# A mixer stage rebuilt with channels on the partitions, and a reordered expert stage

## The reference

```
x = x + attention(norm(x))   # 16 heads, top 128 of 512 scores kept, three powers
x = x + experts(norm(x))     # 8 experts, capacity 512 tokens each
x = x + mixer(norm(x))       # a state space mixer
x = x + experts(norm(x))     # the same weights again
```

```
z, xBC, dt = split(u W_in)                      # 128, 160 and 8 columns
dt = softplus(dt + dt_bias)
x, B, C = split(silu(causal_conv4(xBC) + conv_b))
a = -exp(A_log) * dt                            # a log decay for each token and head
y[l] = sum_{s<=l} (C[l].B[s]) exp(sum_{s<r<=l} a[r]) dt[s] x[s]   # for each head
y = concat(y + D x, z)                          # 256 channels
y = (y - mean) / sqrt(var + 1e-5) * ln_w + ln_b
out = y W_out.T
```

## Time and profile before

| what | us |
|---|---|
| median of three runs | 2978.61 |
| the profiled execution: its time | 2989.87 |
| the profiled execution: its span | 2988.0 |
| attention and set-up, up to about | 2347 |
| first experts, about | 2347 to 2480 |
| mixer, about | 2480 to 2899 |
| second experts, about | 2899 to 2988 |

### The profile page before, as it was taken

One profiled execution on the slowest core, in us unless ns is written; L12 is line 12 of the kernel. 1 busy time (PEld: TensorE's weight loads), 2 busy tenths in 40 slices (PEclk: granted clock), 3 DMA queues, 4 the chain that ended last, 5 costly groups with the idle time before them and its releaser, 6 DMA issues. The chain is left out here.

```text
span 2988.0 us, 55735 instructions
## 1 busy us (share of the span) xinstructions
PE 2555.0 (86%) x16480; PEld 1495.8 (50%) x16480; DVE 2633.9 (88%) x6567; ACT 2087.5 (70%) x6347; POOL 2273.3 (76%) x2876
## 2 busy tenths in 40 slices
PE   5888888888888888888988888888887786889868
PEld 3444444444444444444444444444444445777754
DVE  7999999999999999999999999999998354655537
ACT  4788888888888888888887888888887253222325
POOL 5899999989999999999999999999998242222205
PEclk7899999999999999999999999999999786655569
DMA  4444444444444444444444444444442000000000
GB/s 130 117 121 118 123 121 120 120 121 121 120 122 119 122 119 124 119 121 119 122 119 121 121 123 118 122 122 120 124 121 82 1 1 15 8 4 4 1 1 29
DMA packets 368965, 281.82 MB, mean 94 GB/s; under 512 B 27726, under 2 KB 366744, under 8 KB 368664
## 3 DMA queue, kind: packets, MB, share of 16 engines
q1 hardware_dynamic: 367736, 276.16, 33.1%
q10 hardware_dynamic: 928, 2.10, 0.2%
HBM read 139.48 MB, written 136.58 MB: 92 GB/s over the span
## 5 line engine op out<-in xcount | busy, mean ns | idle before, releaser
L969 DVE MAX8 top<-work 128x8 f32<-128x512 f32 x1536 | 995.3, 701 | 0.0
L978 DVE MATCH_REPLACE8 work<-top,work 128x512 f32<-128x512 f32 x1024 | 695.7, 698 | 0.0
L1055 POOL TENSOR_TENSOR scores<-scores,cut 128x512 f32<-128x512 f32 x512 | 642.0, 1276 | 0.0
L588 PE MATMUL bank<-probs_t,u 128*64 128x512 f32 x2048 | 473.3, 604 | 11.3 <-ACT u L824 1.4
L1047 POOL TENSOR_SCALAR cut<-scores,minus_max_and_least 128x512 f32<-128x512 f32 x512 | 354.2, 692 | 46.9
L876 ACT ACTIVATE probs_of_tile<-scores,minus_max_and_least 128x512 f32<-128x512 f32 x512 | 376.3, 767 | 13.1 <-POOL scores L1055 13.1
L1068 POOL TENSOR_SCALAR probs_of_tile<-probs_of_tile,inverse 128x512 f32<-128x512 f32 x512 | 349.4, 693 | 26.9 <-DVE inverse L935 1.4
L978 DVE MATCH_REPLACE8 work<-top,scores 128x512 f32<-128x512 f32 x512 | 347.8, 698 | 0.0
L966 DVE MAX8 top<-scores 128x8 f32<-128x512 f32 x512 | 330.8, 699 | 1.8 <-ACT scores L817 1.5
L1051 POOL TENSOR_SCALAR cut<-cut 128x512 f32<-128x512 f32 x512 | 305.7, 613 | 21.5
L795 ACT ACTIVATE band<-band 128x129 f32<-128x129 f32 x512 | 155.2, 304 | 224.5 <-DMA band<-probs_scratch 224.2
(11 more groups left out here) (269 smaller groups left out, 5089.4 us busy)
## 6 DMA issues: line engine op xcount, KB each, us to landing
probs_scratch<-probs_of_tile SPq DMA_DIRECT2D x256, 256.0 KB, 2.5
band<-probs_scratch SPq DMA_DIRECT2D x256, 256.0 KB, 3.2
rel_scratch<-rel SPq DMA_DIRECT2D x256, 254.0 KB, 3.1
relj<-rel_scratch SPq DMA_DIRECT2D x256, 128.0 KB, 2.3
relj<-rel_scratch SPq DMA_DIRECT2D x512, 64.0 KB, 2.5
stream<-in_L_attn_a_x SPq DMA_DIRECT2D x4, 512.0 KB, 8.3
mixer_xs<-stream_normed_t SPq DMA_DIRECT2D x8, 256.0 KB, 2.7
out_stream<-stream SPq DMA_DIRECT2D x8, 256.0 KB, 2.3
```

Of the source, the lines that this page charges most:

```text
L588: last = nc.tensor.matmul(U[HEADS[h], lo:hi], lhs, pt[mpar][:, h, jt, lo:hi], start=(jt == 0 and lo == 0), stop=(jt == NT - 1 and step > 0))
L969: nc.vector.max(top[q][:, h, 8 * rnd:8 * rnd + 8], work[:, h, :]).then_inc(s.next_tops, 1)
L978: nc.vector.match_replace(out=work[:, h, :], in_to_replace=top[q][:, h, 8 * rnd:8 * rnd + 8], in_values=sc[Tc][:, h, :] if rnd == 0 else w ...
L1055: nc.gpsimd.tensor_tensor(sc[Tc][:, h, :], sc[Tc][:, h, :], cut[:, h, :], ALU.add).then_inc(s.masked, 1)
```

## The change

The attention stage is not touched.

**Experts.** The gates of group i+1 are turned and copied after tile 2 of group i, not at the start of group i+1. The turn of the normed stream of group i-2 moves from the group's start to behind tile 1, its copy by ScalarE likewise, and its logits from behind tile 2 to behind tile 3. A copy's own semaphore becomes a link of the chain.

```diff
@@ experts, TensorE
             for i in range(GROUPS):
-                if i:
-                    pe.wait_ge(g_kept, i)
...
-                last.then_inc(g_turned, 1)
-                if follow and i >= 2:
-                    late(i - 2)
+                if i == 0:
+                    turn_gates(0)
...
-                    if c == 2 and follow and i >= 2:
+                    if c == 1 and follow and i >= 2:
+                        late(i - 2)
+                    if c == 2 and i + 1 < GROUPS:
+                        turn_gates(i + 1)
+                    if c == 3 and follow and i >= 2:
                         group_products(nc, pe, follow, i - 2, follow.W, k.XNT, EIGHT)
```

```diff
@@ first_half: log decays
-                for h in range(MH):
-                    last = nc.tensor.matmul(DF[h // 4][:, (h % 4) * P:(h % 4 + 1) * P], al[q][:, h, :], r.upto[:, :],
+                for e in range(2):
+                    last = nc.tensor.matmul(DF[e][:, :], r.after[:, :],
+                                            al[q][:, 4 * e:4 * e + 4, :].rearrange("p h t -> p (h t)"),
                                             start=True, stop=True)
@@ second_half: y as channels by tokens, 32 stationary columns a head
-                for h in range(MH):
-                    nc.tensor.matmul(Y[:, h * MP:(h + 1) * MP], mm[q][:, h, :], dx[q][:, h, :], start=True, stop=True)
-                nc.tensor.matmul(Y[:, P:2 * P], cs[par][:, cols], st[:, :, :].rearrange("n h p -> n (h p)"),
-                                 start=True, stop=True)
+                if c < NT - 1:
+                    nc.tensor.matmul(SO[0:MS, chunk(c)], bt[q][:, :], xd[q][:, :, :].rearrange("s h p -> s (h p)"),
+                                     start=True, stop=True)
                 for h in range(MH):
+                    to = slice(32 * (h // 2), 32 * (h // 2) + 32)
+                    last = nc.tensor.matmul(Y[to, chunk(c)], dx[q][:, h, :], mm[q][:, h, :],
+                                            start=(h % 2 == 0), stop=(h % 2 == 1))
+                last.then_inc(m.y_made, 1)
@@ once a batch
+            def from_states(j):
+                pe.wait_ge(m.states, 5 * j + 5)
+                for c in range(1, NT):
+                    last = nc.tensor.matmul(SO[:, chunk(c)], st[j % 2][:, c - 1, :], cs[j % 2][:, chunk(c)],
+                                            start=True, stop=True)
+            def from_start(j):
+                for c in range(1, NT):
+                    last = nc.tensor.matmul(PB[:, chunk(c)], wide[:, c - 1, :], r.upto[:, :], start=True, stop=True)
+            def mean(j, front):
+                nc.tensor.matmul(PZ[:, :], shares[:, :], yt[j % 2][:, :], start=True, stop=False)
+                nc.tensor.matmul(PZ[:, :], shares[:, :], zt[j % 3][:, :], start=False, stop=True).then_inc(m.moments, 1)
+            def square_sums(j):
+                for c in range(NT):
+                    for e in range(2):
+                        last = nc.tensor.matmul(PZ[:, c:c + 1], sq[e][:, chunk(c)], r.ones[:, 0:1],
+                                                start=(e == 0), stop=(e == 1))
```

More of the change, by code:

```diff
@@ L1255, in _, with turn_gates @@
         def _(pe):
[L1256 to L1260, removed]
+            def turn_gates(i):
                 if i:
@@ new lines, in turn, with logits @@
+            def turn(j, front):
+                if front is not None:
+                    pe.wait_ge(m.starts_kept, front + 1)
+                elif j:
+                    pe.wait_ge(m.logits_kept, j)
+                group_turn(nc, pe, follow, j, gw.xn[:, j % 2, :], PB, k.ident, 1)
+            def logits(j):
+                pe.wait_ge(follow.kept, j + 1)
+                for c in range(NT):
+                    t = j * NT + c
+                    last = nc.tensor.matmul(PB[:, c * E:(c + 1) * E], k.XNT[:, t * P:(t + 1) * P], follow.W,
+                                            start=True, stop=True)
+                last.then_inc(follow.products, 1)
@@ L1680, in body @@
                 if front is not None:
-                    projected(front, 1 - par)
-                for c in range(2):
-                    if back is not None:
-                        keep_turned(back, c)
-                    if cur is not None:
-                        decays(cur, c + 2)
+                    keep_starts(front)
+                if cur is not None:
+                    decays(cur, 2)
+                if done is not None:
+                    group_keep(nc, act, follow, done, PB, k.XNT)
@@ L1687, in body @@
+                if cur is not None:
+                    decays(cur, 3)
                 if front is not None:
                     squash(front)
[L1689 to L1694 removed]
+                if done is not None:
                     act.wait_ge(follow.products, done + 1)
[L1696 to L1697 removed]
@@ L1819, in body @@
+            def body(front, cur, back, done):
                 if cur is not None:
-                    nc.vector.memset(st[:, :, :], 0.0)
-                    before(0)
-                    before(1)
+                    before(cur, 0)
+                    before(cur, 1)
+                if back is not None:
+                    center(back)
                 if front is not None:
                     convolution(front)
-                for c in range(NT):
-                    if cur is not None:
-                        n = behind(c)
-                        if c + 2 < NT:
-                            before(c + 2)
-                    if back is not None and c + 1 < NT:
-                        into_stream(c)
@@ L1852, in body @@
+                if cur is not None:
+                    before(cur, 2)
+                    before(cur, 3)
+                    states(cur)
                 if back is not None:
-                    into_stream(NT - 1)
-                    dve.wait_ge(m.out_added, (back + 1) * NT)
-                    group_merge(nc, dve, follow, gw, k.X, back)
+                    variance(back)
                 if front is not None:
-                    silu(front, 1 - par)
+                    silu(front)
+                if back is not None:
+                    into_stream(back)
@@ L1858, in body @@
                 if cur is not None:
[L1859 to L1866 removed]
+                    add_up(cur)
```

535 lines of the change are left out of this document (278 added, 257 removed).

## The result

The changed kernel takes 2866.55 us (median of 4 runs, 2862.98 to 2867.54) against 2977.64 for the kernel before (2975.43 to 2992.16): ratio 0.9615, 95% interval 0.9583 to 0.9647, some 111 us faster. The forecast was 2837, in a range of 2806 to 2900. The sign and the range held; the gain was 30 us smaller than forecast.

The account below looks back on a forecast made before the run. TensorE, mostly at its low 1.2 GHz clock, and its waits were taken as the bound. Mixer -117, tables +1 and experts -26.5 gave -142: 2978.6 - 142 = 2837 us, range 2806 to 2900.

Parts of the forecast that it names:

- The experts: First experts, groups 2 to 7: 10.1 us a group once the wait before the turn goes; -26.5 us in all.
- The tables and the start-up: Before the mixer's first transpose: tables +1 us; start-up from 17 to 15 us without the copies by DMA.
- Rival 1: Mixer: TensorE stays at 1.2 GHz, a full step takes 58.5 us, the kernel 3028, slower; chance 0.08.
- The step: Steady mixer step between first transposes of batches: 29.3 + 3 (clock) + 1.2 (waits) = 33.5 us, range 31 to 37.
- waits: Steady mixer step: VectorE's convolution, slowed by GpSimd, ends some 5 us late against 3 us of slack; 1.2 us.
- TensorE's work at 2.4 GHz: Steady mixer step: TensorE's work, 58.5 us in cold units, takes 29.3 us if all runs at 2.4 GHz.
- cost of the low clock: Steady mixer step: time added by TensorE's fall to the low level; 3 us.
- one fall of some 6 to 8 us in each [step], at a cost of 3 to 4: Mixer step: high clock for most of it, with one fall behind the narrow square sums and logits at its end.
- Rival 3: Mixer: the clock falls repeatedly, half the step low, 41 us a step, 2897 us in all; chance 0.16.
- my own list: Signs: steps of 33 to 34 us, mixer clock above 0.85, no experts' wait; wrong if the clock stays below 0.7.
- y was priced at 12.2 cold: Mixer, y's 64 products of a batch in four column groups: 13 slots of 16, 12.2 us at 1.2 GHz, or -1.5.
- The mixer's sum: Whole mixer, start-up, batches 0 to 7 and tail: from 409 to 292 us, -117.

Follow-up runs that it names:

- the kernel with whole columns: Changed kernel with dt*x zero-padded to 128 stationary columns for each head, so no y products run side by side: 2853.53 us, ratio 0.9562.
- that of 2812 us: Changed kernel with the layer norm's squares on ScalarE instead of GpSimd and square sums moving 128 columns instead of one: 2812.16 us, ratio 0.9442.

## Why the prediction came out as it did

**What held.** The experts: 9.9 us a group for 10.1 forecast, no wait before the turn, -29 for -26.5. The tables and the start-up to 1 us. That TensorE and its clock, not the other engines, bound the old mixer: shown by the old kernel with a wide y. Rival 1 (3028) needed the clock low throughout; it is low for half of the step. The convolution is stretched where GpSimd squares, as the rows of after show, and moving the squares removes 3.2 us of it. The Trainium skill's rule that was weighed there ("SBUF — State Buffer", section "Who interferes with whom": the exclusive lock of the shared port pair) agrees with these runs: 2.38 us for what is 0.73 alone, and the stretch follows GpSimd's bias where it was moved. The prediction counted only VectorE's instructions with two SBUF sources; one with a single source is stretched too, the second of the convolution, which takes 1.26 us beside GpSimd's square of y and 0.47 with the squares on ScalarE.

**The step was forecast at 33.5 us and took 37.7, by errors that partly cancel.** It lies beyond the 31 to 37 that the prediction gave it. Its three terms, measured in the step of 37.7 us with clock 0.73: the capacity at the high level is 0.73 x 37.7 = 27.5 us, less the wait of 3.7, which lies mostly at that level, makes 23.8 of work; the low stretch costs (1 - 0.73) x 37.7 = 10.2; waits 3.7.

| term | forecast | measured | error |
|---|---|---|---|
| TensorE's work at 2.4 GHz | 29.3 | 23.8 | -5.5 |
| cost of the low clock | 3 | 10.2 | +7.2 |
| waits | 1.2 | 3.7 | +2.5 |
| step | 33.5 | 37.7 | +4.2 |

That the time fell into the range of 2806 to 2900 is in part luck. With TensorE's work as dear as forecast and the rest as measured, a step would have taken 5.5 us more; my estimate from these rows is 8 x 5.5 = 44 us, so some 2910.

**The term that failed: "one fall of some 6 to 8 us in each [step], at a cost of 3 to 4".** There is one fall in each step, but it begins some 3 us before the square sums behind which it was put, with the wait of 3.68 us, and it lasts 20 us. I had the rows for it: in the first batch the clock stayed low through the following wide log decays (3.78), and I let it rise within a few microseconds. The runs show which part of the change would have shortened it. With the wait cut to 0.89 us, or filled to 0.56, the clock of a step stays at 0.75 to 0.86; with the square sums widened and the wait left in, it is at 0.89 to 0.94 from batch 2 on. They don't show that the narrow sums do it alone: in batch 7, behind no wait, they run at the high level, and in two steps of the kernel with whole columns they do so behind waits of 1.06 and 0.52 us. Widening costs nothing in itself, as the prediction's own prices had it (a product of 16 columns costs nearly what one of 128 costs), and I did not draw the conclusion for the kernel after. Rival 3, half of the step low for "the narrow square sums and logits and any new wait", had the mechanism with a chance of 0.16, and its clock is what was measured; its 2897 was too high since the work was smaller. By my own list the mixer's clock above 0.85 was to show the forecast right; it was 0.73, between that and the 0.7 that would have made it wrong.

**y was priced at 12.2 cold, and is about 4.** I took it that only neighbours in different column groups run together, from products that alternate between two halves. Sixteen instructions in four groups take 0.59 us at the high level and 1.02 at the low one, from start to start of what follows, four times a batch 2.4 or 4.1. That is 3.7 us of the -5.5 at the high level; the log decays, 7.1 for 7.85, are another 0.7, and the rest is spread thinly. Where the columns are whole, the same block takes 2.05. The Trainium skill's warning that was weighed ("TensorEngine Tiling (Array Packing)", section "Key Properties": a drain at each change of the mode) is not seen: the products ahead of the block give way to it after 0.23 us (0.33 where the columns are whole), and whatever the drain costs is inside these 0.23 and 0.59 us.

**The wait was priced 1 to 2 us and is 3.68.** The convolution ends 5.8 us later than alone, for 5 forecast, so the stretch was sized well and the slack (3 us) too large: of the 5.8 only 2.1 were covered. TensorE, with two y blocks ahead of it that are each 0.9 us cheaper than priced, arrives earlier; in the run with the dear y 1.06 were left.

**Batches and the sum.** Batches 2 to 6 took 186 for 167.5 (5 x 3.7 us more a step) and batches 0 and 1 took 67 for 59.5, where waits of 5.61 and 3.88 us on the same pieces stand. Batch 7 and the tail took 47 for 50. The mixer's sum is -94 for -117.

**The other 11 us.** I worked with the profiled execution of before, 2989.9, and took 11.3 off to reach the median. Forecast in that execution's own terms was 2848, and the profiled execution of after took 2866.4, a miss of 18. But the median of after is 2866.6, the same. What explains it is that the old kernel's 11 us were long steps of the old mixer, a part of what the change removed in that execution, so that the kernel after has no such excess to take off. The run of the experts alone, whose old mixer was 18 us shorter with the same code, speaks for it; it is one trace, and no second trace of the kernel before shows it.

**What stays open.** What starts the fall: the long wait was never taken out whole with the narrow square sums left in (0.89 and 0.52 us remained), and batch 7 has less work around them besides. Why the clock falls in some steps and not in others with the same code, in the kernel with whole columns and in that of 2812 us; whether widening the logits as well would bring anything (in the kernel with wide sums they run at the high level already, 1.06 us); and how much of the step y's narrowness alone, without the other edits of the mixer, had cost in the new order.

## What to carry to other kernels

Count a narrow product by what may happen to the clock around it, not only by its own time: where one column costs the same as 128, try 128. Look at the single steps, since the clock of one need not be that of the next. Where VectorE and GpSimd both read two operands in SBUF, moving one of GpSimd's instructions moved the stretch, and only giving it to another engine took it away. And when a profiled execution lies above the median, look where its excess is before you subtract it from a forecast: if the change removes that place, it doesn't carry over.

## What the runs showed that was not expected

- Sixteen MATMUL instructions in four groups of 32 stationary columns, 128 moving columns each: 0.59 us at 2.4 GHz, where 16 undivided ones take 2.05.
- Square sums with 128 moving columns in place of one: 31 us less in the whole kernel (2835.4 for 2866.6); y of the old kernel with 128 in place of 16: 47 us less (2930.9 against 2978).
- An unneeded block of 28 instructions (3.3 us) in a wait made the kernel 9 us faster, at the edge of what can be told, and padding y to four times its stationary columns 13 us, though the second's runs spread over 30 us and reach the changed kernel's time.
- The same 16 instructions with one moving column, in the same kernel, at the low level in every step with a wait before them and at the high level in batch 7 (0.56 and 0.36 us a pair).
- ScalarE's squares of 512 columns take 0.63 us each; GpSimd's took 1.22 and 1.88 beside VectorE and 1.04 in the tail.
